# Scattering expert rows with addition into one DRAM row per token

## The chip, the cores and the metric

The kernel runs on 1 core of one Trainium2 chip. The metric is the device time of one execution in microseconds (us); lower is better. A run of the kernel before takes 539.44 us (median of 3 runs, 538.76 to 542.75).

## The reference

The input x is 8 sequences of 512 tokens with 256 numbers each, 4096 tokens in all. After a layer norm, two branches run on the same normed rows `xn`: a gated linear recurrence with its projections, whose result is `s`, and a mixture of 8 experts, of which each token uses two.

```python
logits = xn @ router_weight.T
top_vals, top_idx = jax.lax.top_k(logits, 2)
top_gates = softmax(top_vals, axis=1)
# for each expert e, with g_e the token's gate for it (0 if not chosen):
h = xn @ w_in[e].T;  a, b = split(h, 2)
acc = acc + g_e * ((silu(a) * b) @ w_out[e].T)
moe = acc + bias
out = x + s * silu(moe)
```

What matters here: each token's row of `moe` is the sum of two gated expert rows and the bias row.

## The kernel before

Engines: PE is the matrix engine, DVE the vector engine, ACT the scalar engine, POOL the general engine that issues indirect DMAs, SP the engine that only issues DMAs and waits.

**First part (0 to about 160 us).** x is loaded, normed and transposed, the tokens are routed, and the recurrence branch runs chunk by chunk (8 chunks of 512 tokens). Meanwhile SP brings in the expert weights in 24 pieces of 512 KB (`load_w`, L298 to L305, L314), POOL scatters every token's normed row twice into a DRAM table sorted by expert, `slots_dram` (64 indirect DMAs of 128 rows, L424). A row there is 256 numbers and 4 of metadata: expert, two parts of the gate, and the token's number in a form that gives the destination row (`tok_row`). Slots without a token are filled with a row whose destination is out of bounds (`NO_ROW`, L370), so that its result is written nowhere.

**Expert part (about 160 to 500 us).** 39 blocks: 32 of 256 slots ("pair blocks", `units(b)` is 2) and 7 of 128 slots ("single blocks"). `b` is the block and `i = b % 2` the half of each double buffer. For a block:
- SP, `load_slots` (L321): waits until `meta` of block b-2 is done (`meta_ready >= b-1`, L324), then loads the block's slots (L326).
- PE, `one_block(b)` (L1143): `hidden` half 0 of block b (into bankA), the transposes of block b+1's slots (L1112, need its load), `hidden` half 1 (bankB), then `outputs` of block b-1 (bankC).
- ACT and DVE apply silu, the product and the split into high and low halves between them.
- DVE, `gate_y(b)` (L917): `ys = outputs * gate + half_bias`, one instruction for each 128 rows (L924), and signals `y_sb`.
- POOL, in program order `meta(b)`, `scatter_y(b-1)`, `meta(b+1)`, `scatter_y(b)`, and so on. `meta(b)` (L442 to L462) waits for `y_scattered[i]`, that is until the scatter of block b-2 has landed (L447), and works out gate and destination of each slot in seven small instructions. `scatter_y(b)` (L464 to L473) waits for `y_sb` and issues one indirect DMA (L470) for each 128 rows into `y_dram`.

`y_dram` has two rows per token, 8192 in all. A token's first choice goes to its even row and its second choice to its odd row. Each of them holds half the bias, so that their sum holds it whole. The half bias is made by a small load and one ACT instruction (L625, L631, L632).

**Tail (about 500 us to the end).** When the last scatters have landed (L349), SP loads `y_dram` in 8 chunks of 1 MB, both rows of each token (L352). For each chunk: DVE adds the two rows (`sum_y`, L957), ACT takes silu (L646), DVE multiplies by `s` (`finish`, L963) and adds x (`add_x`, L970), SP stores 512 KB (L355). DVE's order is sum 0, sum 1, finish 0, sum 2, finish 1, add 0, and so on.

Of the kernel before, what the change touches and what calls it, by code (L numbers as in the profile page):

```python
# [43 lines left out]
BLOCK = 256  # L44
SB = BLOCK // P
# [8 lines left out]
META = 4  # L54
# [13 lines left out]
MASKED = -3.0e38  # L68
ROWS_OUT = TOPK * T
NO_ROW = float(ROWS_OUT + 1)  # L70
N_SCATTERS = TOPK * NT
# [12 lines left out]
def units(b):  # L84

    return SB if not isinstance(b, int) or b < PAIRS else 1


def scatters_before(b, i):

    if not isinstance(b, int):
        return b if i == 0 else b - 1
    return sum(units(a) for a in range(i, b, 2))


def build(nc, x, wq, wv, wg, wo, beta, ln_g, ln_b, router, w_exp, bias, out):
    ctx = ExitStack()
    with ctx:
# [3 lines left out]
        def sem(name):  # L102
            return ctx.enter_context(nc.semaphore(name))
# [3 lines left out]
        y_dram = nc.dram_tensor("y_dram", (ROWS_OUT, D), F32).ap()  # L107
# [4 lines left out]
        w_raw = sb("w_raw", [P, E * EW])  # L112
# [4 lines left out]
        rows_raw = sb("rows_raw", [P, NT * ROW])  # L117
# [11 lines left out]
        def part(raw, words):  # L129
            at[0] += words  # L130
            return raw[:, at[0] - words:at[0]]

        def recurrence_buffers(raw):
# [19 lines left out]
              for _ in range(2)]  # L153
# [6 lines left out]
        ys = [part(rows_raw, SB * D).rearrange("p (s d) -> p s d", d=D) for _ in range(2)]  # L160
        half_bias = part(rows_raw, D)
        is_first, gate_c, dest_f = [[part(rows_raw, SB) for _ in range(2)] for _ in range(3)]
        dest = [part(rows_raw, SB).bitcast(I32) for _ in range(2)]
# [3 lines left out]
        at[0] = 0  # L167
        y_in = [part(w_raw, TPC * TOPK * D).rearrange("p (t c d) -> p t c d", t=TPC, c=TOPK)
                for _ in range(CH)]
        x_late = part(w_raw, (CH - X_EARLY) * TPC * D).rearrange("p (t d) -> p t d", d=D)  # L170
        assert at[0] <= E * EW
        res = [a[:, :, 0, :] for a in y_in]

# [22 lines left out]
        tok_row = routing((NT,), "t")  # L196
# [17 lines left out]
        fill32 = sb("fill32", [P, ROW])  # L214
# [23 lines left out]
        def slots_ps_of(b, i):  # L238
# [3 lines left out]
        x_loaded = [sem(f"x_loaded{i}") for i in range(2)]  # L242
        rt_loaded, wat_loaded, cols_loaded, bias_loaded = map(
            sem, ("rt_loaded", "wat_loaded", "cols_loaded", "bias_loaded"))
# [3 lines left out]
        lam_th, lam_ready, bias_halved = sem("lam_th"), sem("lam_ready"), sem("bias_halved")  # L248
        wat_hi_ready, wat_lo_ready = sem("wat_hi_ready"), sem("wat_lo_ready")
# [22 lines left out]
        y_loaded = [sem(f"y_loaded{c}") for c in range(CH)]  # L272
        moe_sum, moe_silu, gated, dve_added = map(
            sem, ("moe_sum", "moe_silu", "gated", "dve_added"))
# [4 lines left out]
        y_v = y_dram.rearrange("(t p c) d -> p t c d", p=P, c=TOPK)  # L279
        slots_v = slots_dram.rearrange("(n p) r -> p n r", p=P)  # L280
# [6 lines left out]
        def _(sp):  # L287
# [16 lines left out]
            for c in range(3):  # L304
                load_w(c)  # L305
# [54 lines left out]
        def _(pool):  # L360
            n = [0]

            def step(ins):

                n[0] += 1
                ins.then_inc(pool_step, 1)
                pool.wait_ge(pool_step, n[0])

            step(pool.memset(fill32[:, :], 0.0))
            step(pool.memset(fill32[:, D + META - 1:D + META], NO_ROW))  # L370
            pool.nop().then_inc(consts, 1)
# [20 lines left out]
            for g in range(AHEAD - 1):  # L392
# [3 lines left out]
                      allow_small_or_imprecise_dtypes=True)  # L396
            pool.iota(tok_row[:, :], [[2 * P, NT]], base=1, channel_multiplier=2,
                      allow_small_or_imprecise_dtypes=True)
# [43 lines left out]
            def meta(b, i, first):  # L442

                pool.wait_ge(slot_loaded[i], b * 8 + 16 if i == 0 else b * 8 + 8)
                if not first:
                    pool.wait_ge(y_sb, b - 1)
                    pool.wait_ge(y_scattered[i], 16 * scatters_before(b, i))  # L447
                e_b = blk_e[:, bass.ds(b, 1)].to_broadcast([P, SB])
                pool.tensor_tensor(is_first[i][:, :], slot_in[i][:, :, D], e_b, ALU.subtract)\  # L449
                    .then_inc(pool_step, 1)  # L450
                pool.wait_ge(pool_step, b * 3 + n_meta + 1)

                pool.tensor_tensor(spare[:, i:i + 1], spare[:, 6:7], spare[:, 6:7], ALU.add)  # L453
# [3 lines left out]
                pool.tensor_tensor(gate_c[i][:, :], slot_in[i][:, :, D + 1], is_first[i][:, :], ALU.mult)  # L457
# [6 lines left out]
            def scatter_y(b, i):  # L464
# [12 lines left out]
            meta(1, 1, True)  # L477
            scatter_y(0, 0)
            with pool.Fori(2, PAIRS - 1, 2) as b:
# [11 lines left out]
        def _(act):  # L491
# [132 lines left out]
            recur(CH - 1, convert=False, last=True)  # L624
            act.dma_start(half_bias, bias).then_inc(bias_loaded, 16)  # L625
            half(0, 0, 0, 0)
# [3 lines left out]
            high_slots(1, 1, True)  # L630
            act.wait_ge(bias_loaded, 16)  # L631
            act.activation(half_bias, half_bias, ACT.Copy, scale=0.5).then_inc(bias_halved, 1)  # L632
            half(1, 1, 0, 1)
# [16 lines left out]
        def _(dve):  # L650
            n = [0]

            def step(ins):

                n[0] += 1
                ins.then_inc(route_step, 1)
                dve.wait_ge(route_step, n[0])
# [283 lines left out]
            halves(1, 1)  # L941
            dve.wait_ge(bias_halved, 1)
            gate_y(0, 0, True)
# [27 lines left out]

            sum_y(0)
            for c in range(CH):
                if c + 1 < CH:
                    sum_y(c + 1)
                finish(c)
                if c >= 1:
                    add_x(c - 1)
# [236 lines left out]
```

## Time and profile before

| what | us |
|---|---|
| time, median of 3 runs | 539.44 |
| time of the profiled execution | 541.56 |
| its span, first to last instruction | 539.7 |
| PE busy | 440.1 |
| DVE busy | 317.6 |
| POOL busy | 235.9 |
| ACT busy | 218.2 |
| last scatter issued | 497.95 |
| first load of `y_dram` issued | 500.50 |
| first instruction of the tail on DVE | 505.93 |
| last instruction of DVE | 534.69 |

The granted clock of TensorE was 0.924 of full speed on average, and full from 200 to 490 us. Times of the rows are counted from the span's start. Busy time is counted per engine, and engines overlap. What sets the time is the chain of work that ended last, in which each piece waited for the one before it.

### The profile page before, as it was taken

Reading aid. Unit: us, or ns where it says so; the run is one execution under the profiler, and the core shown is the slowest. Engines: PE = TensorE matmul, PEld = TensorE weight load, DVE = VectorE, ACT = ScalarE, POOL = GpSimd, SP = SyncE. Lnnn points to the kernel's source line nnn. Section 1 sums busy time; section 2 is a strip of 40 time slices with the busy share of each in tenths; the row PEclk is TensorE's granted clock in tenths of the full one; section 3 lists DMA queues with packets and bytes.
Section 4 is the critical chain, followed back from the end, with each engine's and each line's share of the span. In section 5 each row is a group of like instructions: output and inputs, shape, how many; then the busy total and the mean of one; then the engine's idle time right before and its main releaser. Section 6 shows DMA issues by size and latency. Waiting matters only on the chain.

```text
span 539.7 us, 12930 instructions
## 1 busy us (share of the span) xinstructions
PE 440.1 (82%) x3798; PEld 352.1 (65%) x3799; DVE 317.6 (59%) x609; ACT 218.2 (40%) x355; POOL 235.9 (44%) x536
## 2 busy tenths in 40 slices
PE   1766796979985999999999999999999997886000
PEld 1643454636544888888888888888888886664000
DVE  4898999969944245454454544545445444332397
ACT  4863366577546233333242332423323332221131
POOL 4717876877832043434444344443444344434000
PEclk9659898989989799999999999999999999999555
DMA  8802539966121214422212122121221211101897
GB/s 263 279 7 100 174 130 304 313 235 227 69 79 49 79 51 127 149 63 95 59 59 68 49 78 59 59 67 49 77 58 60 63 47 56 36 22 27 300 386 259
DMA packets 40824, 63.83 MB, mean 118 GB/s; under 512 B 4701, under 2 KB 29536, under 8 KB 40800
## 3 DMA queue, kind: packets, MB, share of 16 engines
q1 hardware_dynamic: 32512, 45.41, 27.0%
q0 software_dynamic: 6480, 16.92, 8.8%
q10 hardware_dynamic: 1808, 1.19, 0.7%
q8 instruction: 14, 0.23, 0.2%
q14 instruction: 10, 0.08, 0.0%
HBM read 40.00 MB, written 24.42 MB: 119 GB/s over the span
## 4 chain that ended last, share of the span: by engine, by line
issue 38%; DMA 23%; POOL 17%; DVE 11%; ACT 4%; PE 3%; POOLq 2%; DVEq 0%; SPq 0%; ACTq 0%
DMA y_dram<-rows_raw 17%; POOL slots_dram L424 3%; POOL y_dram L470 2%; DVE w_raw L848 2%; PE bankC L988 2%; DMA w_raw<-y_dram 2%; DMA work<-w_exp_in 2%; DMA w_raw<-x_in 2%; ACT w_raw L561 2%; POOL rows_raw L461 1%; POOL spare L453 1%; POOL rows_raw L449 1%; POOL spare L468 1%; POOL rows_raw L457 1%; POOL rows_raw L454 1%
## 5 line engine op out<-in xcount | busy, mean ns | idle before, releaser
L988 PE MATMUL bankA<-rows_raw,w_raw 128*128 128x256 f16 (+1 forms) x936 | 105.6, 268 | 7.2 <-DVE rows_raw L904 5.7
L988 PE MATMUL bankC<-w_raw,rows_raw 128*128 x852 | 100.1, 273 | 5.0 <-issue 5.0
L988 PE MATMUL bankB<-rows_raw,w_raw 128*128 128x256 f16 (+1 forms) x936 | 103.7, 264 | 0.1
L988 PEld LDWEIGHTS bankA<-rows_raw,w_raw 128*128 x936 | 87.3, 99 | 21.0 <-issue 9.2
L988 PEld LDWEIGHTS bankB<-rows_raw,w_raw 128*128 x936 | 86.8, 97 | 11.0 <-issue 0.2
L988 PEld LDWEIGHTS bankC<-w_raw,rows_raw 128*128 128x128 f16 x852 | 81.3, 98 | 18.1 <-issue 7.3
L424 POOL DMA_INDIRECT slots_dram<-rows_raw,pos_i x64 | 74.6, 1166 | 29.9 <-issue 18.5
L470 POOL DMA_INDIRECT y_dram<-rows_raw x71 | 72.5, 1021 | 30.7 <-issue 30.7
L914 DVE TENSOR_TENSOR rows_raw<-rows_raw 128x512 f16<-128x512 f32 (+1 forms) x78 | 50.3, 645 | 52.4 <-ACT rows_raw L613 52.4
L910 DVE SCALAR_TENSOR_TENSOR rows_raw<-rows_raw,bankA 128x512 f32<-128x512 f32 (+1 forms) x39 | 25.0, 640 | 93.9 <-ACT rows_raw L608 93.9
L608 ACT ACTIVATE rows_raw<-bankA 128x512 f32<-128x512 f32 (+1 forms) x39 | 21.8, 559 | 130.4 <-PE bankA L988 130.4
L613 ACT ACTIVATE rows_raw<-rows_raw 128x512 f16<-128x512 f32 (+1 forms) x78 | 46.1, 591 | 56.2 <-DVE rows_raw L910 56.2
L468 POOL TENSOR_TENSOR spare<-spare 128x1 f32<-128x1 f32 x39 | 7.5, 193 | 105.4 <-DVE rows_raw L924 105.3
L910 DVE SCALAR_TENSOR_TENSOR rows_raw<-rows_raw,bankB 128x512 f32<-128x512 f32 (+1 forms) x39 | 25.0, 640 | 21.6 <-ACT rows_raw L608 21.5
L924 DVE SCALAR_TENSOR_TENSOR rows_raw<-bankC,rows_raw 128x256 f32<-128x256 f32 x71 | 31.4, 480 | 7.0 <-PE bankC L988 4.1
L449 POOL TENSOR_TENSOR rows_raw<-rows_raw,blk_e 128x2 f32<-128x2 f32 x39 | 7.7, 197 | 61.0 <-DMA y_dram<-rows_raw 61.0
L608 ACT ACTIVATE rows_raw<-bankB 128x512 f32<-128x512 f32 (+1 forms) x39 | 21.8, 559 | 28.7 <-PE bankB L988 28.7
L848 DVE SCALAR_TENSOR_TENSOR w_raw<-work,w_raw 128x1024 f32 (+1 forms) x24 | 27.8, 1215 | 1.1 <-ACT w_raw L561 0.9
L1112 PE MATMUL bankD<-ident,rows_raw 128*128 128x128 f32 x138 | 22.4, 281 | 5.4 <-DMA rows_raw<-slots_dram 5.1
L904 DVE TENSOR_TENSOR rows_raw<-bankD,rows_raw 128x512 f16<-128x512 f32 (+1 forms) x38 | 24.1, 635 | 2.6 <-ACT rows_raw L600 2.6
L561 ACT ACTIVATE w_raw<-work 128x1024 f32 (+1 forms) x24 | 23.8, 1048 | 4.3 <-DMA work<-w_exp_in 4.3
L588 ACT ACTIVATE work<-bankD,stat 128x256 f32<-128x256 f32 x32 | 15.4, 563 | 19.3 <-POOL stat L389 19.3
(160 smaller groups left out, 604.7 us busy)
## 6 DMA issues: line engine op xcount, KB each, us to landing
work<-w_exp_in SPq DMA_DIRECT2D x24, 512.0 KB, 5.4
rows_raw<-slots_dram SPq DMA_DIRECT2D x32, 260.0 KB, 2.7
w_raw<-y_dram SPq DMA_DIRECT2D x8, 1024.0 KB, 13.5
w_raw<-x_in SPq DMA_DIRECT2D x9, 512.0 KB, 4.5
out<-w_raw SPq DMA_DIRECT2D x8, 512.0 KB, 4.2
work<-x_in SPq DMA_DIRECT2D x7, 512.0 KB, 4.4
slots_dram<-fill SPq DMA_DIRECT2D x9, 260.0 KB, 5.9
y_dram<-rows_raw POOLq DMA_INDIRECT x71, 2.5
```

The source lines that it names most:

```text
L424: pool.indirect_dma_start(out=slots_dram, out_offset=bass.IndirectOffsetOnAxis(slot, 0), in_=row, in_offset=None, bounds_check=SLOTS - 1, ...
L470: pool.indirect_dma_start(out=y_dram, out_offset=bass.IndirectOffsetOnAxis(dest[i][:, s:s + 1], 0), in_=ys[i][:, s, :], in_offset=None, bo ...
L561: act.activation(w_hi[:, bass.ds((c * PIECES + i) * PIECE, PIECE)], wst[:, i % STAGES, :], ACT.Copy, scale=WSCALE).then_inc(w_hi_ready, 1)
L608: act.activation(sil[j][:, :, 0:n], AB[j][:, :, 0:n], ACT.Silu, scale=1.0 / WSCALE).then_inc(sil_ready, 1)
L613: act.activation(g_hi[i][:, 2 * j:2 * j + 2, 0:n], g32[j][:, :, 0:n], ACT.Copy)\
L848: dve.scalar_tensor_tensor(w_lo[:, piece], wst[:, i % STAGES, :], WSCALE, w_hi[:, piece], ALU.mult, ALU.subtract).then_inc(w_lo_ready, 1)
L904: dve.tensor_tensor(xT[i][:, KD:2 * KD, 0:n], slots_ps_of(b, i)[:, :, 0:n], xT[i][:, 0:KD, 0:n], ALU.subtract).then_inc(slot_lo_ready, 1)
L910: dve.scalar_tensor_tensor(g32[j][:, :, 0:n], sil[j][:, :, 0:n], 1.0 / WSCALE, AB[j][:, :, BLOCK:BLOCK + n], ALU.mult, ALU.mult).then_inc( ...
L914: dve.tensor_tensor(g_lo[i][:, 2 * j:2 * j + 2, 0:n], g32[j][:, :, 0:n], g_hi[i][:, 2 * j:2 * j + 2, 0:n], ALU.subtract).then_inc(g_split, 1)
L924: last = dve.scalar_tensor_tensor(ys[i][:, s, :], bankC[:, i, s * D:s * D + D], gate_c[i][:, s:s + 1], half_bias, ALU.mult, ALU.add)
L988: last = pe.matmul(out_ap, lhsT, rhs, start=(n == 0), stop=(n == len(todo) - 1))
L1112: last = pe.transpose(slots_ps_of(b, i)[:, k, s * P:s * P + P], slot_in[i][:, s, k * P:k * P + P], ident32[:, :])
```

## The change

- `y_dram` gets one row per token (4096) and 128 more rows at the end for slots without a token: 4224 rows. `tok_row` is the token's number, and the filler row's destination is 4096 plus its partition, made by an iota in place of a memset.
- After the first 4 pieces of weights, SP sets all of `y_dram` to the bias with 5 DMAs from DRAM to DRAM.
- `gate_y` leaves the bias out: it becomes a product with a per-row scalar. The load and the scaling of `half_bias` go.
- `meta` loses the instruction that subtracts `is_first` from the destination (L458), since both choices go to the same row.
- `scatter_y` adds into DRAM (`compute_op=ALU.add`), with `oob_is_err=True`. A scatter now waits until the scatter of the block before it has landed as well (`y_scattered[1 - i]`), and the first one until the bias is in place. Two additions into one row must not overlap.
- In the tail a chunk of `y_dram` is 512 KB. `sum_y` is gone, and ACT waits for the load itself.

```diff
+            load_w(0)
+            for t in range(0, NT, 2 * TPC):
+                sp.dma_start(y_v[:, t:t + 2 * TPC, :], bias.unsqueeze(1).to_broadcast([P, 2 * TPC, D]))\
+                  .then_inc(y_started, 16)
+            sp.dma_start(y_v[:, NT, :], bias).then_inc(y_started, 16)
+            for c in range(1, 3):
                 load_w(c)
...
             for c in range(CH):
-                sp.dma_start(y_in[c], y_v[:, c * TPC:(c + 1) * TPC, :, :]).then_inc(y_loaded[c], 16)
+                sp.dma_start(res[c], y_v[:, c * TPC:(c + 1) * TPC, :]).then_inc(y_loaded[c], 16)
...
-                pool.tensor_tensor(dest_f[i][:, :], slot_in[i][:, :, D + 3], is_first[i][:, :], ALU.subtract)\
...
-                pool.tensor_copy(dest[i][:, :], dest_f[i][:, :]).then_inc(meta_ready, 1)
+                pool.tensor_copy(dest[i][:, :], slot_in[i][:, :, D + 3]).then_inc(meta_ready, 1)
...
+            def scatter_y(b, i, first=False):
                 pool.wait_ge(y_sb, b + 1)
                 pool.wait_ge(meta_ready, b + 1)
+                if first:
+                    pool.wait_ge(y_started, 16 * (NT // (2 * TPC) + 1))
+                else:
+                    pool.wait_ge(y_scattered[1 - i], 16 * scatters_other(b, i))
...
                     pool.indirect_dma_start(
                         out=y_dram, out_offset=bass.IndirectOffsetOnAxis(dest[i][:, s:s + 1], 0),
-                        in_=ys[i][:, s, :], in_offset=None,
-                        bounds_check=ROWS_OUT - 1, oob_is_err=False).then_inc(y_scattered[i], 16)
+                        in_=ys[i][:, s, :], in_offset=None, bounds_check=ROWS_OUT - 1,
+                        oob_is_err=True, compute_op=ALU.add).then_inc(y_scattered[i], 16)
...
-                act.wait_ge(moe_sum, c + 1)
+                act.wait_ge(y_loaded[c], 16)
...
-                    last = dve.scalar_tensor_tensor(ys[i][:, s, :], bankC[:, i, s * D:s * D + D],
-                                                    gate_c[i][:, s:s + 1], half_bias,
-                                                    ALU.mult, ALU.add)
+                    last = dve.tensor_scalar(ys[i][:, s, :], bankC[:, i, s * D:s * D + D],
+                                             gate_c[i][:, s:s + 1], None, ALU.mult)
...
-            def sum_y(c):
-                dve.wait_ge(y_loaded[c], 16)
-                dve.tensor_tensor(res[c], y_in[c][:, :, 0, :], y_in[c][:, :, 1, :], ALU.add)\
-                   .then_inc(moe_sum, 1)
```

## Rows read from the trace of the kernel before

**Rows 1.** Page, busy time of each engine: us, share of span, instructions.
```profile
PE 440.1 (82%) x3798; PEld 352.1 (65%) x3799; DVE 317.6 (59%) x609; ACT 218.2 (40%) x355; POOL 235.9 (44%) x536
```

**Rows 2.** Page, the chain that ended last: shares of the span.
```profile
issue 38%; DMA 23%; POOL 17%; DVE 11%; ACT 4%; PE 3%; POOLq 2%; DVEq 0%; SPq 0%; ACTq 0%
```

**Rows 3.** Chain in order of time, 337 to 366 us: start, length, what.
```profile
346.30 2.42 DMA y_dram<-rows_raw
...
349.80 0.15 POOL rows_raw L458
...
350.34 2.42 issue
```

**Rows 4.** Timeline, 340 to 366 us and SP from 347: start, length, instruction, [idle before].
```profile
343.26 0.88 DVE L924 SCALAR_TENSOR_TENSOR rows_raw<-bankC,rows_raw 128x256 f32<-128x256 f32 x2
345.70 0.42 PEld L1112 LDWEIGHTS bankD<-ident,rows_raw 128*128 128x128 f32 x4 [0.24 <-DMA rows_raw<-slots_dram]
354.04 0.47 PEld L1112 LDWEIGHTS bankD<-ident,rows_raw 128*128 128x128 f32 x4
360.13 0.88 DVE L924 SCALAR_TENSOR_TENSOR rows_raw<-bankC,rows_raw 128x256 f32<-128x256 f32 x2
...
351.21 0.38 SPq L326 DMA_DIRECT2D rows_raw<-slots_dram  x1
```

**Rows 5.** DMA issues by line: KB each, median us to landing; queue q0's total.
```profile
q0 software_dynamic: 6480, 16.92, 8.8%
...
rows_raw<-slots_dram SPq DMA_DIRECT2D x32, 260.0 KB, 2.7
out<-w_raw SPq DMA_DIRECT2D x8, 512.0 KB, 4.2
work<-x_in SPq DMA_DIRECT2D x7, 512.0 KB, 4.4
rows_raw<-slots_dram SPq DMA_DIRECT2D x7, 130.0 KB, 2.1
```

**Rows 6.** Page, groups of instructions: count, busy us, mean ns, idle before.
```profile
L424 POOL DMA_INDIRECT slots_dram<-rows_raw,pos_i x64 | 74.6, 1166 | 29.9 <-issue 18.5
L470 POOL DMA_INDIRECT y_dram<-rows_raw x71 | 72.5, 1021 | 30.7 <-issue 30.7
```

**Rows 7.** Timeline from 470 us: single blocks, the last scatters, the tail.
```profile
470.19 0.42 DVE L910 SCALAR_TENSOR_TENSOR rows_raw<-rows_raw,bankA 128x256 f32<-128x256 f32 x1 [2.46 <-ACT rows_raw L608]
...
496.10 1.04 POOL L470 DMA_INDIRECT y_dram<-rows_raw  x1 [0.52 <-issue]
...
497.25 0.18 POOL L468 TENSOR_TENSOR spare<-spare 128x1 f32<-128x1 f32 x1
497.95 0.99 POOL L470 DMA_INDIRECT y_dram<-rows_raw  x1 [0.51 <-issue]
500.50 13.07 SPq L352 DMA_DIRECT2D w_raw<-y_dram  x8
505.93 1.23 DVE L957 TENSOR_TENSOR w_raw<-w_raw 128x1024 f32<-128x1024 f32 x1 [8.77 <-DMA w_raw<-y_dram]
507.19 1.06 ACT L646 ACTIVATE w_raw<-w_raw 128x1024 f32<-128x1024 f32 x1 [13.22 <-DVE w_raw L957]
...
522.21 1.22 DVE L957 TENSOR_TENSOR w_raw<-w_raw 128x1024 f32<-128x1024 f32 x1
...
525.61 1.22 DVE L957 TENSOR_TENSOR w_raw<-w_raw 128x1024 f32<-128x1024 f32 x1
...
534.69 1.23 DVE L970 TENSOR_TENSOR w_raw<-w_raw 128x1024 f32<-128x1024 f32 x1
```

**Rows 8.** Stretches: length, busy of each engine, PEclk, DMA share, GB/s.
```profile
30.00:45.00 15.00, 12.21 (x170) 8.64 (x170) 12.99 (x34) 6.21 (x11) 4.09 (x4) 0.74 0.08 28
510.00:520.00 10.00, 0.00 (x0) 0.00 (x0) 9.63 (x10) 3.17 (x3) 0.00 (x0) 0.50 1.05 388
```

**Rows 9.** Waits of SP's own queue: us in total, times, longest.
```profile
SPq L302 <- DVE w_raw L848: 86.3, 16, 40.5
```

More of the change, by code:

```diff
@@ L68 @@
 MASKED = -3.0e38
-ROWS_OUT = TOPK * T
-NO_ROW = float(ROWS_OUT + 1)
+ROWS_OUT = T + P
 N_SCATTERS = TOPK * NT
@@ L93, in scatters_before, with scatters_other @@
     return sum(units(a) for a in range(i, b, 2))
+def scatters_other(b, i):
+    if not isinstance(b, int):
+        return b if i == 0 else b + 1
+    return sum(units(a) for a in range(1 - i, b, 2))
 def build(nc, x, wq, wv, wg, wo, beta, ln_g, ln_b, router, w_exp, bias, out):
@@ L160, in build @@
         ys = [part(rows_raw, SB * D).rearrange("p (s d) -> p s d", d=D) for _ in range(2)]
-        half_bias = part(rows_raw, D)
-        is_first, gate_c, dest_f = [[part(rows_raw, SB) for _ in range(2)] for _ in range(3)]
+        is_first, gate_c = [[part(rows_raw, SB) for _ in range(2)] for _ in range(2)]
         dest = [part(rows_raw, SB).bitcast(I32) for _ in range(2)]
@@ L167, in build @@
         at[0] = 0
-        y_in = [part(w_raw, TPC * TOPK * D).rearrange("p (t c d) -> p t c d", t=TPC, c=TOPK)
-                for _ in range(CH)]
+        res = [part(w_raw, TPC * D).rearrange("p (t d) -> p t d", t=TPC) for _ in range(CH)]
         x_late = part(w_raw, (CH - X_EARLY) * TPC * D).rearrange("p (t d) -> p t d", d=D)
         assert at[0] <= E * EW
-        res = [a[:, :, 0, :] for a in y_in]
         def x_of(c):
@@ L242, in build @@
         x_loaded = [sem(f"x_loaded{i}") for i in range(2)]
-        rt_loaded, wat_loaded, cols_loaded, bias_loaded = map(
-            sem, ("rt_loaded", "wat_loaded", "cols_loaded", "bias_loaded"))
+        rt_loaded, wat_loaded, cols_loaded, y_started = map(
+            sem, ("rt_loaded", "wat_loaded", "cols_loaded", "y_started"))
         wst_loaded = [sem(f"wst_loaded{i}") for i in range(STAGES)]
@@ L247, in build @@
         rt_hi, rt_split = sem("rt_hi"), sem("rt_split")
-        lam_th, lam_ready, bias_halved = sem("lam_th"), sem("lam_ready"), sem("bias_halved")
+        lam_th, lam_ready = sem("lam_th"), sem("lam_ready")
         wat_hi_ready, wat_lo_ready = sem("wat_hi_ready"), sem("wat_lo_ready")
@@ L272, in build @@
         y_loaded = [sem(f"y_loaded{c}") for c in range(CH)]
-        moe_sum, moe_silu, gated, dve_added = map(
-            sem, ("moe_sum", "moe_silu", "gated", "dve_added"))
+        moe_silu, gated, dve_added = map(sem, ("moe_silu", "gated", "dve_added"))
         stored = sem("stored")
@@ L278, in build @@
         out_v = out.rearrange("(t p) d -> p t d", p=P)
-        y_v = y_dram.rearrange("(t p c) d -> p t c d", p=P, c=TOPK)
+        y_v = y_dram.rearrange("(t p) d -> p t d", p=P)
         slots_v = slots_dram.rearrange("(n p) r -> p n r", p=P)
@@ L303, in load_w @@
                         "p a w -> p (a w)")).then_inc(wst_loaded[i % STAGES], 16)
-            for c in range(3):
+            load_w(0)
[4 more added lines that the diff above has]
+            for c in range(1, 3):
                 load_w(c)
@@ L369, in _ @@
             step(pool.memset(fill32[:, :], 0.0))
-            step(pool.memset(fill32[:, D + META - 1:D + META], NO_ROW))
+            step(pool.iota(fill32[:, D + META - 1:D + META], [[1, 1]], base=T, channel_multiplier=1,
+                           allow_small_or_imprecise_dtypes=True))
             pool.nop().then_inc(consts, 1)
@@ L396, in _ @@
                       allow_small_or_imprecise_dtypes=True)
-            pool.iota(tok_row[:, :], [[2 * P, NT]], base=1, channel_multiplier=2,
+            pool.iota(tok_row[:, :], [[P, NT]], base=0, channel_multiplier=1,
                       allow_small_or_imprecise_dtypes=True)
@@ L456, in meta @@
                 pool.wait_ge(pool_step, b * 3 + n_meta + 2)
-                pool.tensor_tensor(gate_c[i][:, :], slot_in[i][:, :, D + 1], is_first[i][:, :], ALU.mult)
-                pool.tensor_tensor(dest_f[i][:, :], slot_in[i][:, :, D + 3], is_first[i][:, :], ALU.subtract)\
+                pool.tensor_tensor(gate_c[i][:, :], slot_in[i][:, :, D + 1], is_first[i][:, :], ALU.mult)\
                     .then_inc(pool_step, 1)
@@ L461, in meta @@
                 pool.tensor_tensor(gate_c[i][:, :], gate_c[i][:, :], slot_in[i][:, :, D + 2], ALU.add)
-                pool.tensor_copy(dest[i][:, :], dest_f[i][:, :]).then_inc(meta_ready, 1)
-            def scatter_y(b, i):
+                pool.tensor_copy(dest[i][:, :], slot_in[i][:, :, D + 3]).then_inc(meta_ready, 1)
+            def scatter_y(b, i, first=False):
                 pool.wait_ge(y_sb, b + 1)
                 pool.wait_ge(meta_ready, b + 1)
+                if first:
+                    pool.wait_ge(y_started, 16 * (NT // (2 * TPC) + 1))
+                else:
+                    pool.wait_ge(y_scattered[1 - i], 16 * scatters_other(b, i))
                 pool.tensor_tensor(spare[:, 2 + i:3 + i], spare[:, 6:7], spare[:, 6:7], ALU.add)
@@ L477, in _ @@
             meta(1, 1, True)
-            scatter_y(0, 0)
+            scatter_y(0, 0, True)
             with pool.Fori(2, PAIRS - 1, 2) as b:
@@ L624, in _ @@
             recur(CH - 1, convert=False, last=True)
-            act.dma_start(half_bias, bias).then_inc(bias_loaded, 16)
             half(0, 0, 0, 0)
@@ L630, in _ @@
             high_slots(1, 1, True)
-            act.wait_ge(bias_loaded, 16)
-            act.activation(half_bias, half_bias, ACT.Copy, scale=0.5).then_inc(bias_halved, 1)
             half(1, 1, 0, 1)
@@ L941, in _ @@
             halves(1, 1)
-            dve.wait_ge(bias_halved, 1)
             gate_y(0, 0, True)
@@ L970, in add_x @@
                 dve.tensor_tensor(res[c], res[c], x_of(c), ALU.add).then_inc(dve_added, 1)
-            sum_y(0)
             for c in range(CH):
-                if c + 1 < CH:
-                    sum_y(c + 1)
                 finish(c)
```

## Prediction

> **What bounds the kernel now.** I read the page's busy times first [rows 1]. PE is busy 82% of the span, and one expects the matrix engine to be the bound. The chain that ended last says otherwise [rows 2]: PE holds 3% of it, POOL 17%, DMA 23%, and "issue" (nobody in the view to wait for) 38%. So I laid out one round of the expert part from the chain in order of time [rows 3] and the timeline [rows 4]. The reader is to follow one loop:
>
> - `gate_y` of a block starts at 343.26 and takes 0.88 for its two instructions.
> - POOL issues the second of its two scatters at 346.30. It lands 2.42 later, at 348.7.
> - `meta` of the block two further on waits for that landing and ends at 350.34.
> - SP waits for that `meta`, and issues the slot load at 351.21, 0.87 later (its wait, and reading the row number).
> - PE starts the transposes that need this load at 354.04, 2.83 after the issue, where a load of this size takes 2.7 to land [rows 5]. That leaves about 0.1. In the other parity PE stands idle for the load: 0.24 before the transposes at 345.70.
> - After the transposes come `hidden` half 1 and `outputs`, and the `gate_y` two blocks after the first starts at 360.13.
>
> The loop is 360.13 - 343.26 = 16.87 us for two blocks, and nothing in it is spare. PE alone would need only some 0.24 less per two blocks. So PE and the round trip through POOL, the scatter's landing, `meta` and SP bind at once. Any time added between `gate_y` and the slot load makes two blocks longer by that time; any time taken out gives at most 0.24. POOL itself is not full: it idles 2.42 after `meta` [rows 3].
>
> How many rounds: block b+4's load hangs on block b's scatter. It holds from about block 2's scatter to block 33's gate, 31 blocks or 15.5 rounds; I count 15, since one parity starts with a few tenths in hand. The single blocks at the end have one scatter each and some 1 us in hand.
>
> The tail is bound elsewhere. 24 DVE instructions of 128x1024 run from 505.93 to 535.92 [rows 7]. In mid tail the sums start at 522.21 and 525.61, so three instructions take 3.40, 1.13 each. DMA is full at the same time, 388 GB/s [rows 8]: after the change one of the two could turn out to be the limit.
>
> **The change part by part.** The durations are of the profiled execution (541.56, span 539.7), 2.1 above the median of 539.44; I put the difference on the median.
>
> *Tail.* Before: first load issued at 500.50, first DVE instruction 5.43 later. After: a chunk is 512 KB instead of 1 MB. Half of it less at 388 GB/s is 1.35, so the first one lands about 4.1 after the first issue, silu takes 1.06, and DVE starts at 5.3. Its 16 instructions take 16 x 1.13 = 18.1, and some 0.3 is lost while the second chunk is awaited. DVE ends at 23.7; before it was 35.4. That is 11.7 less; I take 11.5. DMA does not take over: 8.4 MB in place of 12.6 MB at 388 GB/s is 21.6, plus the first landing less than the 27.3 that the tail then lasts. Loads with rows of 1 KB could run slower than these of 2 KB; x comes in with 1 KB rows, and its 512 KB take 4.4 like the 4.2 of the stores [rows 5].
>
> *New wait at the end.* In the loop the wait for the other half's scatter costs nothing: POOL's program has `meta(b+1)` between `scatter_y(b-1)` and `scatter_y(b)`, and it waits for that very landing already. Only the last scatter has no `meta` before it. Before, it went out at 497.95, while the one before was still under way (issued 496.10). After, it waits until 496.10 + 2.55 = 498.65 and then takes the 0.70 from the small addition at 497.25 to the scatter [rows 7]: 499.35. That is +1.4, and behind it are queued the loads of all the tail. It also shows two landings bare, so an addition's extra landing time counts there twice.
>
> *Addition instead of writing.* No row shows it. Two unknowns: e, the longer issue on POOL, and d, the later landing. Per round of a pair block e counts twice and d once.
> - Lowest: both zero. The bytes that POOL handles are the same.
> - e highest: the issue takes twice as long, +1.0 on 1.02 [rows 6]. Nearest row: the same instruction with other rows and more going on around it, L424, takes 1.17, +0.15. I take 0.15.
> - d highest: the old rows are first read, then added and written. A read of 130 KB takes 2.1 from issue to landing [rows 5]. If the read runs beside the source's, 130 KB more cost what 260 KB cost over 130 KB in the same load, 2.7 - 2.1 = 0.6. Reading DRAM instead of writing it makes 4.4 from 4.2, +0.2. I take 0.8.
> - So 2 x 0.15 + 0.8 = 1.1 per round, and 0.95 for a single scatter.
>
> A third way to d: by queue q0's total [rows 5], 131 KB took 8.8% x 539.7 x 131 / 16920 = 0.37 us of all engines. If an addition only moves the read bytes twice, the landing comes 0.37 later and the round grows by 2 x 0.15 + 0.37 = 0.67, 0.52 for a single scatter; the sum is then 15 x 0.42 - 11.5 + 1.4 + 1.04 = -2.8. I take 0.8 since a load's landing grew by more than its bytes.
>
> The Trainium skill ("Collectives: The Full Stack", section "The bandwidth ceiling: the fold count and why AG ≠ RS ≠ AR") says that a reducing DMA is slower because it reads two sources, not because of the adding. By that it would be 536.6 in place of 544.0. No row of the kernel before shows an adding DMA.
>
> *Taken out of the round.* L458 is 0.15 on POOL [rows 3]. `gate_y` reads one operand less: 0.88 for two, while a DVE instruction with 256 numbers takes 0.42 at the least in the rows [rows 7], so 0.05, up to 0.1. Together 0.25 at best, which I take.
>
> *Hidden.* SP's five bias DMAs write 4.3 MB. They stand ahead of the second group of weights, which is held up to 40.5 us by DVE anyway [rows 9], and DMA is at 0.08 of its capacity from 30 to 45 us [rows 8]; 4.3 MB read and written are at most 22 us at 388 GB/s. Without that cover it would be these 22 us. The first expert scatter, which waits for them, comes over 100 us later. `half_bias` on ACT, iota for memset, 896 filler rows more written: nothing, they lie beside a busy PE or a scatter that is issued anyway.
>
> **The sum.** Per round 1.1 - 0.25 = +0.85, times 15 = +12.8. Tail -11.5, new wait +1.4, twice 0.95 = +1.9. In all +4.6: 539.4 + 4.6 = 544.0. The gain in the tail is paid back in the loop. It turns at a round extra of about 0.8, below which the kernel is faster.
>
> **Rivals.**
> 1. *Adding is nearly free* (extra below 0.7 per round). For it: the small share of DMA in the loop, the same number of indices. With zero: the round can shrink by only 0.24, -3.6; -11.5 + 1.4 - 3.6 = -13.7, 525.7. With the bytes read twice and no more, 0.67: -2.8, 536.6; 0.10 of this rival's chance. At 0.7 (single 0.6): 6.75 - 10.1 + 1.2 = -2.2, 537.2. This ends on the other side and decides from 0.8 down.
> 2. *Adding is dear* (above 1.5): each row is read, added and written in its own turn, or POOL prepares half as many entries again. At 1.5 (single 1.25): 18.75 - 10.1 + 2.5 = +11.2, 550.6. At read-then-write, 2.1 + 0.3 = 2.4: 32.3 - 10.1 + 4.5 = +26.7, 566. Against it: POOL's 2.42 idle says that even then no second loop closes.
> 3. *The loop does not bind* because SP's load could be late by more than I read: PE's 0.24 idle would come from something else. Then only the tail counts: -11.5 + 1.4 + 1.9 = -8.2, 531.2. Against it: the transposes follow the load by 2.7 to 2.8 in both parities, the time of its landing.
>
> **From chances to numbers.** Forecast (extra 0.7 to 1.5: 537.2 to 550.6) 0.45; rival 1 0.27; rival 2 0.20; rival 3 0.08. A change under 1% (5.4 us) is not told from none in this kernel. Faster than 534.0 needs an extra below 0.47: two thirds of rival 1 and all of rival 3, with some rounding 0.27. Slower than 544.8 begins at 1.16: rival 2 and nearly half of the forecast, 0.40. Within: 0.33. The range for 8 in 10 goes from 529 (an extra of 0.2) to 559 (an extra of 2.0). For the forecast alone it is 537 to 551.
>
> **What the new profile would show.** Two `gate_y` of one parity 17.7 apart instead of 16.87; the scatter's landing at about 3.3 to 3.4 after its issue instead of 2.42; the DMA_INDIRECT at 1.15 to 1.2; PE idle before the transposes, over 0.5 per block. In the tail no DVE sum, 16 instructions, and 27 to 28 from the first load's issue to the end. The last scatter goes out only after the one before has landed. I am wrong if the landing stays near 2.4 (rival 1), if it is past 4 (rival 2), if the landing is late and the period is not (rival 3), or if the tail's DMA keeps DVE waiting.

## The result and the profile after

| | before | after |
|---|---|---|
| time, median (range) | 540.14 (538.76 to 542.75) | 583.12 (576.84 to 589.49) |
| time of the profiled execution, its span | 541.56, 539.7 | 581.51, 579.7 |
| ratio to before, with its interval | | 1.0749 [1.0672, 1.0827] |

The run of 589.49, over 1.5% above the fastest of its kernel, is left out of the ratio and of the comparisons below; the other three have a median of 581.51. The change makes the kernel 7.5% slower, about 41 us. The forecast was slower by 4.6 us, with a range up to 559, so the sign is right and the size is far off.

The page of the changed kernel, busy times first, then the slices, the costliest groups, and the DMA issues (us to landing last):

```profile
PE 458.6 (79%) x3798; PEld 364.3 (63%) x3799; DVE 309.5 (53%) x601; ACT 219.4 (38%) x354; POOL 274.7 (47%) x497
...
PEclk9998897998898999998899889889999999898855
...
L482 POOL DMA_INDIRECT y_dram<-rows_raw x71 | 113.0, 1592 | 30.7 <-issue 30.7
...
L1111 PE MATMUL bankD<-ident,rows_raw 128*128 128x128 f32 x138 | 23.5, 291 | 36.8 <-DMA rows_raw<-slots_dram 36.0
...
w_raw<-y_dram SPq DMA_DIRECT2D x8, 512.0 KB, 7.5
```

POOL's indirect DMA takes 1.59 us instead of 1.02 [rows 6]. PE, which hardly ever waited for a slot load before, now waits 36.0 us for them. Its busy time has grown by 18.5 us with the same number of matmuls, and PEclk shows an 8 again and again through the loop where it was 9: it computes more slowly as well as later.

One round of the loop [rows 3, 4] in the changed kernel. First the chain in order of time:

```profile
333.08 3.69 DMA y_dram<-rows_raw
...
341.40 3.65 DMA y_dram<-rows_raw
```

The landing comes 3.65 to 3.69 after the second scatter's issue, against 2.42. Over all 71 scatters, the least, the median and the most from issue to landing, before and then after:

```profile
DMA to landing us min/median/max: 2.2/2.5/3.7
...
DMA to landing us min/median/max: 3.6/3.8/5.1
```

Then the timeline of the same stretch:

```profile
329.53 0.88 DVE L933 TENSOR_SCALAR rows_raw<-bankC,rows_raw 128x256 f32<-128x256 f32 x2
...
331.18 1.59 POOL L482 DMA_INDIRECT y_dram<-rows_raw  x1 [0.51 <-issue]
...
332.28 2.78 PE L987 MATMUL bankB<-rows_raw,w_raw 128*128 128x256 f16 x24
...
333.08 1.58 POOL L482 DMA_INDIRECT y_dram<-rows_raw  x1 [0.31 <-issue]
...
336.95 0.18 POOL L457 TENSOR_TENSOR rows_raw<-rows_raw,blk_e 128x2 f32<-128x2 f32 x1 [2.28 <-DMA y_dram<-rows_raw]
337.21 0.65 POOL L461 TENSOR_TENSOR spare<-spare 128x1 f32<-128x1 f32 x1
...
342.43 0.45 PEld L1111 LDWEIGHTS bankD<-ident,rows_raw 128*128 128x128 f32 x4 [2.40 <-DMA rows_raw<-slots_dram]
...
343.06 4.31 PE L987 MATMUL bankB<-rows_raw,w_raw 128*128 128x256 f16 x24
```

The second scatter goes out 1.90 after the first (1.37 before, up to the issue at 346.30 in [rows 3]), PE waits 2.40 for the slot load, and then 24 matmuls into bankB take 4.31, where the same 24 took 2.78 one block earlier. The small addition at L461, a part of `meta`, takes 0.65 here in an even block and 0.20 in the odd block after it. The stretches of the same time, with the granted clock as the third number from the right, before DMA's share and GB/s:

```profile
332.00:335.00 3.00, 3.00 (x30) 2.72 (x28) 1.47 (x3) 1.71 (x3) 2.36 (x2) 1.00 0.37 44
343.00:346.00 3.00, 3.00 (x16) 2.11 (x15) 0.82 (x2) 0.60 (x1) 0.56 (x3) 0.50 0.40 49
347.00:350.00 3.00, 3.00 (x30) 2.70 (x28) 1.26 (x2) 1.23 (x2) 0.00 (x0) 1.00 0.33 89
```

After the idle stretch the granted clock is 0.50, 1.2 GHz, and then it is full again, 2.4 GHz. This one costs 4.31 - 2.78 = 1.53 us, on top of the wait.

The tail, from the timeline:

```profile
542.35 1.62 POOL L482 DMA_INDIRECT y_dram<-rows_raw  x1 [0.51 <-issue]
542.98 0.41 SPq L354 DMA_DIRECT2D w_raw<-x_in  x1
542.98 0.48 DVE L933 TENSOR_SCALAR rows_raw<-bankC,rows_raw 128x256 f32<-128x256 f32 x1 [1.41 <-PE bankC L987]
547.60 0.18 POOL L480 TENSOR_TENSOR spare<-spare 128x1 f32<-128x1 f32 x1 [3.63 <-DMA y_dram<-rows_raw]
548.30 1.56 POOL L482 DMA_INDIRECT y_dram<-rows_raw  x1 [0.52 <-issue]
552.10 7.26 SPq L359 DMA_DIRECT2D w_raw<-y_dram  x8
...
557.31 1.23 DVE L965 TENSOR_TENSOR w_raw<-w_raw,xs_raw 128x1024 f32<-128x1024 f32 x1 [13.84 <-ACT w_raw L655]
...
574.72 1.22 DVE L972 TENSOR_TENSOR w_raw<-w_raw 128x1024 f32<-128x1024 f32 x1
```

Where the 39.95 us between the two profiled executions are, by points of the timelines:

| part | before | after | difference |
|---|---|---|---|
| start to the gate of block 2 | 207.48 | 210.15 | +2.7 |
| gate of block 2 to gate of block 33 | 259.77 | 301.80 | +42.0 |
| gate of block 33 to that of block 38 | 29.43 | 31.03 | +1.6 |
| last gate to the first load of the tail | 3.82 | 9.12 | +5.3 |
| first load of the tail to the end | 39.2 | 27.6 | -11.6 |

### The profile page after: what moved, and what is told of

Same layout as the page of the kernel before. It is cut to its first block, busy times and chain, and to the rows that moved or that the text cites. A ratio compares the mean times of both kernels' runs of the same rounds, so it can differ in the third digit from the quotient of the medians.

```text
span 579.7 us, 12886 instructions
## 1 busy us (share of the span) xinstructions
PE 458.6 (79%) x3798; PEld 364.3 (63%) x3799; DVE 309.5 (53%) x601; ACT 219.4 (38%) x354; POOL 274.7 (47%) x497
## 3 DMA queue, kind: packets, MB, share of 16 engines
q0 software_dynamic: 13296, 17.83, 18.1%
## 4 chain that ended last, share of the span: by engine, by line
issue 33%; DMA 28%; POOL 17%; DVE 10%; PE 7%; POOLq 2%; ACT 1%; DVEq 0%; SPq 0%; ACTq 0%
DMA y_dram<-rows_raw 26%; PE bankC L987 2%; POOL y_dram L482 2%; POOL spare L461 2%; POOL slots_dram L432 2%; PE bankA L987 2%; DVE w_raw L857 2%; DMA w_raw<-x_in 2%; POOL rows_raw L457 1%; POOL stat L396 1%; POOL rows_raw L465 1%; POOL rows_raw L462 1%; POOL spare L480 1%; DVE work L848 1%; DVE w_raw L965 1%
## 5 line engine op out<-in xcount | busy, mean ns | idle before, releaser
L482 POOL DMA_INDIRECT y_dram<-rows_raw x71 | 113.0, 1592 | 30.7 <-issue 30.7
L987 PE MATMUL bankB<-rows_raw,w_raw 128*128 128x256 f16 (+1 forms) x936 | 117.3, 287 | 0.1
L987 PEld LDWEIGHTS bankB<-rows_raw,w_raw 128*128 x936 | 95.0, 107 | 16.5 <-issue 0.3
L987 PEld LDWEIGHTS bankC<-w_raw,rows_raw 128*128 128x128 f16 x852 | 82.7, 98 | 15.8 <-issue 5.4
L432 POOL DMA_INDIRECT slots_dram<-rows_raw,pos_i x64 | 71.7, 1120 | 30.8 <-issue 20.7
L1111 PEld LDWEIGHTS bankD<-ident,rows_raw 128*128 128x128 f32 x138 | 15.5, 143 | 42.3 <-DMA rows_raw<-slots_dram 41.8
L933 DVE TENSOR_SCALAR rows_raw<-bankC,rows_raw 128x256 f32<-128x256 f32 x71 | 31.4, 479 | 5.8 <-PE bankC L987 5.4
L857 DVE SCALAR_TENSOR_TENSOR w_raw<-work,w_raw 128x1024 f32 (+1 forms) x24 | 27.6, 1213 | 0.0
L612 ACT ACTIVATE rows_raw<-bankD 128x512 f16<-128x512 f32 (+1 forms) x38 | 20.8, 548 | 14.8 <-PE bankD L1111 14.6
```

The lines of the kernel that those rows point to most:

```text
L432: pool.indirect_dma_start(out=slots_dram, out_offset=bass.IndirectOffsetOnAxis(slot, 0), in_=row, in_offset=None, bounds_check=SLOTS - 1, ...
L482: pool.indirect_dma_start(out=y_dram, out_offset=bass.IndirectOffsetOnAxis(dest[i][:, s:s + 1], 0), in_=ys[i][:, s, :], in_offset=None, bo ...
L612: act.activation(xT[i][:, 0:KD, 0:n], slots_ps_of(b, i)[:, :, 0:n], ACT.Copy)\
L857: dve.scalar_tensor_tensor(w_lo[:, piece], wst[:, i % STAGES, :], WSCALE, w_hi[:, piece], ALU.mult, ALU.subtract).then_inc(w_lo_ready, 1)
L933: last = dve.tensor_scalar(ys[i][:, s, :], bankC[:, i, s * D:s * D + D], gate_c[i][:, s:s + 1], None, ALU.mult)
L987: last = pe.matmul(out_ap, lhsT, rhs, start=(n == 0), stop=(n == len(todo) - 1))
```

## The experiments

In the table "loop" is the time from the gate of block 2 to that of block 33 (259.8 before, 301.8 after), a round is two blocks, and a slow round is one of 19.8 us or more, of the 13 between the gates of blocks 4 and 30; the usual round is the median of the others. Loops and rounds are of one profiled execution each. The kernel before took 539.8 to 540.6 beside them.

| kernel | time | ratio to before | usual round | slow rounds | loop |
|---|---|---|---|---|---|
| before | 540.1 | | 16.9 | 0 | 259.8 |
| after | 581.5 | 1.075 | 18.8 | 8 | 301.8 |
| write instead of add | 531.1 | 0.983 [0.979, 0.987] | 16.9 | 0 | 260.5 |
| short filler | 547.7 | 1.014 [1.011, 1.018] | 17.2 | 0 | 265.3 |
| long filler | 560.2 | 1.035 [1.032, 1.039] | 18.1 | 1 | 278.6 |
| double filler | 570.8 | 1.057 [1.050, 1.063] | 18.3 | 1 | 287.4 |
| filler in even blocks | 590.0 | 1.091 [1.085, 1.096] | 18.8 | 9 | 304.3 |
| no wait in the loop | 582.8 | 1.082 [1.075, 1.090] | 18.9 | 7 | 302.0 |
| flag off (one run) | 570.4 | | 18.8 | 4 | 294.7 |
| split loads, added | 525.2 | 0.972 [0.968, 0.976] | 16.6 | 0 | 251.5 |
| split loads, old scatter | 531.1 | 0.984 [0.979, 0.989] | 16.6 | 0 | 251.4 |
| split loads, write instead of add | 521.9 | 0.967 [0.962, 0.972] | 16.6 | 0 | 251.5 |
| split loads, x load last | 524.0 | 0.969 [0.966, 0.972] | 16.6 | 0 | 252.3 |

**1. The addition taken out.**

```diff
-                        oob_is_err=True, compute_op=ALU.add).then_inc(y_scattered[i], 16)
+                        oob_is_err=True).then_inc(y_scattered[i], 16)
```

> This kernel is the changed one with the addition taken out of the scatter: it writes its rows (the output lacks one of each token's two expert rows and the bias). All waits, the bias DMAs, the short tail and the bounds flag stay. Theory A (the addition itself is the cost: 0.57 us longer on POOL per indirect DMA, and a later landing): the issue falls back from 1.59 to about 1.0, the landing from 3.7 to 2.4, a round of two blocks from 18.6 to 20.5 back to 16.7 to 16.9, no half clock between 200 and 490 us, and the time is 540.1 - 11.6 + 1.4 + up to 1.7 for a later start = about 531. Rival B (the bounds flag or the 128 more rows make the issue long): issue still 1.5 to 1.6, time 560 to 583. Rival C (the new waits or the bias DMAs cost): issue short, but time above 540.

The lines of its page:

```profile
PEclk9659898999899899999999999999999999999855
...
L482 POOL DMA_INDIRECT y_dram<-rows_raw x71 | 73.2, 1031 | 30.9 <-issue 30.9
```

and the summary of its scatters, from issue to landing:

```profile
DMA to landing us min/median/max: 2.4/2.5/4.6
```

531.1, as theory A gave. All 50 us between this kernel and the changed one come from adding in place of writing; the waits, the bias DMAs, the flag and the 128 more rows are in both. The short tail then brings what it promised.

**2. The same delay without any addition.** In `meta`, behind the small addition at L453, a filler that nobody reads:

```diff
+                pool.iota(delay, [[1, 860]], base=0, channel_multiplier=0,
+                          allow_small_or_imprecise_dtypes=True)
```

> This kernel is the one before with a filler instruction on POOL in each block's meta, about 1.75 us long (an iota over 860 numbers that nobody reads). Nothing is added in DRAM, the tail is the old one. It puts the same delay into the round trip as the addition does (1.8 us per two blocks). Theory A (the loop binds, and the idle PE then loses its clock): the round grows from 16.87 to at least 18.5, the granted clock falls to half for some 3.4 us in many rounds as in the changed kernel, and the time is 540.1 + 15.5 x 1.75 = 567 without the clock, 575 to 585 with it. Rival B (the delay alone explains everything and the clock belongs to something else): 567 with full clock. Rival C (the loop has slack): under 545.

> As the long delay, but the filler is about 0.7 us long (340 numbers). Theory A (linear in the delay, and the clock falls only from some idle time on): round 17.5, time 540.1 + 15.5 x 0.7 = 551, clock full from 200 to 490 us. Rival B (any added idle makes the clock fall): 555 to 565 with half clock in many rounds. Rival C (slack in the loop): under 543.

The filler was shorter than I had reckoned, 0.85 us and, with 340 numbers, 0.42. So the long one doesn't match the addition's delay, and neither kernel gave its forecast time. What they do show is the slope. With the short one `meta` took 0.4 longer, a round grew by about 0.33 and the loop by 5.6. With the long one `meta` of an even block took 2.8 instead of 1.45 (the filler, and a slower instruction behind it), a round grew by 1.2 and the loop by 18.8, that is 15.5 x 1.2 = 18.6. So the loop has only some 0.1 us of slack per round, and what goes beyond it counts in full. Between the gates of blocks 4 and 30 the clock stayed full but for one round.

**3. The double filler.** The same filler twice in each `meta`.

> This kernel is the one before with two fillers on POOL in each block's meta, each the 860-number iota that took 0.85 us in the long delay and made a round 1.2 us longer (16.87 to 18.1). Nothing is added in DRAM. Theory A (an idle of 2 us of PE before the transposes, whoever causes it, lets its clock fall, as in the changed kernel): the round grows to about 19 and PE idles 2 us or more once a round; then the clock is at half for 3.4 us in most rounds, and a round is over 20.5; time 575 to 595. Rival B (the half clock of the changed kernel comes from the additions' DMA work or from chance): rounds of 19 with full clock, 540.2 + 15.5 x 2.1 = 573 or less.

570.8. The time is rival B's, but the condition that was to be tested did not come about: the usual round was 18.3, and PE's wait fell on both blocks of a round.

```profile
332.63 0.42 PEld L1117 LDWEIGHTS bankD<-ident,rows_raw 128*128 128x128 f32 x4 [1.32 <-DMA rows_raw<-slots_dram]
341.41 0.42 PEld L1117 LDWEIGHTS bankD<-ident,rows_raw 128*128 128x128 f32 x4 [0.55 <-DMA rows_raw<-slots_dram]
```

Only one of the 13 rounds was slow. A round that is 1.5 us longer doesn't by itself bring the clock down.

**4. The filler in even blocks alone.** A power of 8 numbers, 1.67 us:

```diff
+                if i == 0:
+                    pool.tensor_tensor(delay, fill32[:, 0:8], fill32[:, 0:8], ALU.pow)
```

> This kernel is the one before with one filler on POOL (a power of 8 numbers, reckoned at 1.9 us from the 1.04 us that 4 take) in the meta of even blocks alone. Nothing is added in DRAM. The double delay spread PE's idle time over both blocks of a round (1.3 and 0.3 us); here it should stand in one stretch of about 2 us before the transposes, as in the changed kernel. Theory A (the long single idle stretch makes the clock fall, once a round): half clock in at least 6 rounds between 200 and 480 us, 576 to 590 us. Rival B (it needs the additions): full clock nearly throughout, round 18.6 to 18.9, 566 to 572 us.

590.0: theory A, without one addition in DRAM. Its page and its timeline:

```profile
PEclk9998898998998998999889989988998899899655
...
L473 POOL DMA_INDIRECT y_dram<-rows_raw x71 | 73.1, 1030 | 30.4 <-issue 30.4
```

```profile
343.43 0.71 PEld L1115 LDWEIGHTS bankD<-ident,rows_raw 128*128 128x128 f32 x4 [2.60 <-DMA rows_raw<-slots_dram]
...
344.34 3.86 PE L991 MATMUL bankB<-rows_raw,w_raw 128*128 128x256 f16 x24
...
353.71 2.78 PE L991 MATMUL bankB<-rows_raw,w_raw 128*128 128x256 f16 x24
```

The scatters are the old ones (1.03 us). PE idles 2.60 in one stretch, and the 24 matmuls after it take 3.86 instead of 2.78. Nine of 13 rounds are slow. So the half clock needs no addition in DRAM; it comes with one long idle stretch of PE in each round. It isn't certain to follow. In the changed kernel the weight loads wait 2.2 to 2.7 in the eight slow rounds and 2.0 to 2.6 in those at full clock, of which this is one, with its stretch:

```profile
404.37 0.42 PEld L1111 LDWEIGHTS bankD<-ident,rows_raw 128*128 128x128 f32 x4 [2.44 <-DMA rows_raw<-slots_dram]
...
404.00:408.00 4.00, 3.63 (x33) 3.30 (x34) 1.38 (x2) 1.22 (x3) 1.45 (x4) 1.00 0.53 61
```

The Trainium skill ("TensorE: Matmul & The Clock Gate", section "HAM oscillation — how this bites in real kernels") describes a matmul kernel whose clock falls again and again because a wait for DMA is repeated in each tile. The changed kernel's trace agrees in its eight slow rounds, with 0.50 granted after the wait of 2.40, and not in the others, with 1.00 granted after the wait of 2.44.

**5. Two parts of the change that could have been the cause.** The wait on the other half's scatter left out, except at the last block:

```diff
-                else:
+                elif isinstance(b, int) and b == BLOCKS - 1:
                     pool.wait_ge(y_scattered[1 - i], 16 * scatters_other(b, i))
```

> This kernel is the changed one without the new wait on the other half's scatter, except at the last block, where it stays. Meta of the next block already waits for that landing, so the order of the additions is the same. Theory A (the new wait costs nothing in the loop): the time of the changed kernel, 583 +- 6. Rival B (the wait costs in every block): faster by more than 10 us.

582.8 against 581.5, and the loop 302.0 against 301.8: the wait costs nothing in the loop, since `meta` of the next block has waited for that landing.

And the flag back to `oob_is_err=False`, with the addition:

> This kernel is the changed one with the bounds flag as before (an index out of bounds would be skipped). Theory A (the addition makes POOL's instruction long): 1.59 us per indirect DMA, time 583 +- 7. Rival B (the flag does): 1.0 to 1.2 us, and a time about 15 x 1 us lower.

```profile
L482 POOL DMA_INDIRECT y_dram<-rows_raw x71 | 113.0, 1592 | 30.8 <-issue 30.8
```

The instruction stays at 1.59: the flag isn't it. The time, 570.4, is a single one, below the 583 +- 7 expected and below the range of the changed kernel. Its usual round is 18.8, as there, but only 4 of the 13 are slow instead of 8. The four missing are worth 4 x 1.7 = 6.8 of the 11 us, and block 2's gate came 3.2 earlier (206.9 against 210.15). Whether the flag plays a part in that, one run can't say.

**6. The loop cut open.** The slot load becomes two. The 256 numbers that PE transposes wait for the buffer alone; the 4 numbers of metadata go to a small tile `slot_m`, with a semaphore of their own, and wait for `meta`:

```diff
                     sp.wait_ge(slot_t_ps, b - 1)
-                    sp.wait_ge(meta_ready, b - 1)
...
-                sp.dma_start(slot_in[i][:, 0:units(b), :], slots_v[:, bass.ds(row, units(b)), :])\
+                sp.dma_start(slot_in[i][:, 0:units(b), :], slots_v[:, bass.ds(row, units(b)), 0:D])\
                   .then_inc(slot_loaded[i], 16)
+                if not isinstance(b, int) or b >= 2:
+                    sp.wait_ge(meta_ready, b - 1)
+                sp.dma_start(slot_m[i][:, 0:units(b), :], slots_v[:, bass.ds(row, units(b)), D:ROW])\
+                  .then_inc(meta_loaded[i], 16)
```

> This kernel is the changed one with the slot load in two: the 256 numbers of each slot are loaded as soon as PE has transposed the buffer's last content, and only the 4 numbers of metadata, in tiles and with a semaphore of their own, wait for meta of block b-2. The scatter's landing and meta are then no longer ahead of PE's transposes. Theory A (the whole loss is the loop through the slot load): POOL's own round of 7.8 us fits below PE's 8.3, blocks go back to 8.3, PE's clock is full from 200 to 490 us, and the time is about 530 (540.1 - 11.6 tail + 5.3 around the last scatters - 0.15 x 31 = 4.5 less in the loop, +1.7 start = 531). Rival B (adding DMAs slow other traffic or POOL becomes the bound): 545 to 575.

> This kernel is the one before with the slot load in two, the metadata apart, as in the split version of the changed kernel; scatter, bias and tail are the old ones. Theory A (the loop through the slot load binds the kernel before as well, by the 0.24 to 0.29 us that PE idles per two blocks, and more around the single blocks): blocks at 8.30, time 540.2 - 4.5 - 1 = about 535. It then also says what the change brings in the tail alone: the split changed kernel took 525.2. Rival C (PE alone bound the kernel before): 540 +- 1. Rival D (the extra small DMAs cost on SP): above 541.

> This kernel is the split version of the changed one with writes in place of additions (its output lacks one expert row of each token and the bias). It prices the additions where the loop no longer carries them. Theory A (only the two bare landings after the last gate still pay): 525.2 - 2 x 1.25 = 522.7. Rival B (POOL's later scatters and the additions' DMA work still cost in the loop): below 520.

With the additions: 525.2, faster than both kernels of the case. Its page and timeline:

```profile
PEclk9659898989989799999999999999999999999755
...
L487 POOL DMA_INDIRECT y_dram<-rows_raw x71 | 113.3, 1596 | 26.0 <-issue 26.0
```

```profile
341.70 0.60 PE L1116 MATMUL bankD<-ident,rows_raw 128*128 128x128 f32 x4
342.13 2.78 PE L992 MATMUL bankB<-rows_raw,w_raw 128*128 128x256 f16 x24
342.93 1.58 POOL L487 DMA_INDIRECT y_dram<-rows_raw  x1 [0.30 <-issue]
344.75 2.78 PE L992 MATMUL bankC<-w_raw,rows_raw 128*128 x24
...
347.14 0.56 POOL L462 TENSOR_TENSOR rows_raw<-rows_raw,blk_e 128x2 f32<-128x2 f32 x1 [2.63 <-DMA y_dram<-rows_raw]
347.37 2.78 PE L992 MATMUL bankA<-rows_raw,w_raw 128*128 128x256 f16 x24
```

The additions are as long as ever, 1.60, and `meta` still waits 2.63 for their landing. But PE goes from one group of 24 matmuls to the next without a gap, at full clock, 8.3 per block. The loop falls from 301.8 to 251.5. I had expected 531: the loop is 3.8 shorter than reckoned, and the start, for which I had added 1.7, is not later than before (block 2's gate at 206.6, 207.5 before).

The kernel before with the same split takes 531.1, 9.5 less than without (I expected 5). The loop is 8.3 shorter: 3.1 from eleven ordinary rounds with 0.28 each, 1.3 from the block before gate 6, beside which x is loaded (9.6, now 8.29), 0.7 from the one before gate 26, and 3.3 from the last blocks of the loop (gates 29 to 32), where the single blocks begin. So the loop bound the kernel before as well. And on top of a kernel in which it doesn't bind, the change brings 531.1 - 525.2 = 5.9 us.

With writes in place of the additions the split kernel takes 521.9 (expected 522.7): the additions still cost 3.3. From the last gate to the first load of the tail it is 9.1 with additions and 6.5 with writes, 2.6 of the 3.3.

**7. The landing before last.**

```diff
             sp.wait_ge(y_ps, BLOCKS)
-            sp.dma_start(x_late, x_v[:, X_EARLY * TPC:, :]).then_inc(x_late_loaded, 16)
...
             for c in range(CH):
                 sp.dma_start(res[c], y_v[:, c * TPC:(c + 1) * TPC, :]).then_inc(y_loaded[c], 16)
+            sp.dma_start(x_late, x_v[:, X_EARLY * TPC:, :]).then_inc(x_late_loaded, 16)
...
+                if c >= X_EARLY:
+                    dve.wait_ge(x_late_loaded, 16)
```

> This kernel is the split version of the changed one with the 512 KB load of the last chunk of x issued after the loads of the tail, and only the last chunk's addition waits for it. In the changed kernel that load is issued at 542.98, 0.6 us after the last scatter but one (542.35), which lands 5.2 us after its issue where the others take 3.6 to 3.8. Theory A (the load delays that landing): it falls to 3.8, 525.2 - 1.3 = 523.9. Rival B (the landing is long for another reason, or the load costs as much at its new place): 525 +- 0.5.

```profile
487.90 1.62 POOL L487 DMA_INDIRECT y_dram<-rows_raw  x1 [0.51 <-issue]
491.96 0.18 POOL L485 TENSOR_TENSOR spare<-spare 128x1 f32<-128x1 f32 x1 [2.44 <-DMA y_dram<-rows_raw]
```

The last scatter but one is now followed 4.06 later by the next instruction; with the load beside it, it was 5.11. So the load did delay the landing, by about 1 us, and from the last gate to the first load of the tail it is 8.0 instead of 9.1. The time is 524.0 (521.5 to 525.8) against 525.2 (523.6 to 527.3). The two intervals overlap, so the gain in the whole is not shown.

## Why the prediction was wrong

Two terms of the sum failed: the longer issue on POOL, e, was put at 0.15 and measured 0.57 (15 x 2 x 0.42 = 13 us), and the half clock of PE behind its repeated wait was not in the sum at all and costs about 14 us. Point by point:

- **What bounds the kernel: right.** The loop through POOL, the landing, `meta` and SP had hardly any slack [rows 3, 4]. The fillers lengthen the loop of the expert part with a slope of about 15.5 per us of round, and the split removes it. Rival 3 (the loop does not bind) fell. The 0.24 that I gave as the most that could be won per round was about right for the ordinary rounds, 16.87 to 16.59, but I had missed what the loop costs in the block next to the loads of x and in its last blocks.
- **The tail: right.** 27.6 from the first load to the end, forecast 27 to 28; DMA didn't take over.
- **The landing as such: right.** I took d = 0.8. The median landing came 1.3 later after the issue (3.8 against 2.5), of which 0.57 is the longer instruction itself, so 0.7 to 0.8 is the rest.
- **The issue: wrong.** I took e = 0.15, from the spread of the same instruction between two lines [rows 6]. It is 0.57, midway between that and the bound of 1.0. The spread was no measure for another kind of work. Per round the extra is 2 x 0.57 + 0.8 = 1.9 instead of 1.1.
- **Taken out of the round: wrong.** `gate_y` takes 0.88 for two as before. Dropping an operand from this DVE instruction, which reads PSUM, saved nothing. `meta` is 0.15 shorter in odd blocks (1.30) but 0.25 longer in even blocks (1.7), since the small addition at L461 takes 0.55 there instead of 0.19; why is open. From a gate to the end of the `meta` that hangs on it, it is now 2.1 longer in even blocks and 1.75 in odd ones. The longer one, less the loop's slack, sets the round: 16.87 to 18.8, that is +1.9 where the sum had +0.85.
- **Rival 2 came, and not by its sign.** The extra of 1.9 lies in its domain, above 1.5, with a chance of 0.20. Its own prices (550.6 at 1.5, 566 at 2.4) make about 557 of 1.9. I had looked for it in a landing past 4; the landing stayed at 3.8, and 1.14 of the extra was in POOL's instructions.
- **The step that was missing: PE's clock.** Of the 42.0 us that the loop grew, 8 slow rounds with 1.7 more than the usual round each are 14, and the other 28 are the rounds at full clock (15 x 1.9). The two kernels with other numbers of slow rounds give the same 28: 34.9 - 4 x 1.7 with the flag off, 44.5 - 9 x 1.8 with the filler in even blocks. I had PE idle over 0.5 in each block; it idled 2.0 to 2.7 in every second one and not in the others. Without the clock the sum would have ended near 566, still above the range. A sum that prices a wait of PE at its length is too low once the wait is long and in one stretch. The times of the changed kernel's runs go with their mean clocks (576.84 at 0.926, 581.51 at 0.919, 584.72 at 0.908); that they differ by their number of slow rounds is not shown.
- **The last scatters: half.** I gave 3.3 for the new wait and the two bare landings; it was 5.3. The wait was mis-sized. I let the landing before last come 2.55 after its issue at 496.10, but in the trace before it took 3.6, beside the 512 KB load of x (from issue to landing):

```profile
DMA to landing us min/median/max: 3.6/3.6/3.6
```

With 3.6 the wait comes to about 2.5 instead of 1.4. The kernels with writes show it without any addition: from the last gate to the first load of the tail 7.45 against 3.8, and 6.5 against 3.9 with split loads, so 2.7 to 3.6. The additions bring 1.7 to 2.6 more, where I had 1.9. In the changed kernel that landing took 5.1, about 1 of it because of the load (experiment 7).

- **Hidden: right as to size, open in part.** Block 2's gate came 2.7 later in the changed kernel, of which the loop already had about 1. In the four other kernels with additions, which have the same bias DMAs, it came at 205.5 to 207.6, and in the kernel with writes, which has them too, at 205.1, before the 207.48 of the kernel before. The bias DMAs cost nothing that can be seen.
- **The forecast with the landing 0.37 later** (the bytes read twice and no more) was further off than mine. The landing grew by 0.7 to 0.8 beyond the issue. The rule of the Trainium skill ("Collectives: The Full Stack", section "The bandwidth ceiling: the fold count and why AG ≠ RS ≠ AR"), that a reducing DMA is slower because of its second read, does not cover the 0.57 on POOL.

With the prices of this profile the sum is 28 (rounds) + 14 (clock) + 1.6 + 2.7 + 5.3 - 11.6 = 40.0, the difference of the profiled executions. Against the forecast of +4.6 the rounds were 15 too low, the clock 14, the single blocks and last scatters together 3.6 and the start 2.7.

Not settled: why an idle stretch of 2.0 to 2.7 us brings the clock down in some rounds and not in others, and whether the flag changes how often.

## What to carry to other kernels

When the chain of waits runs through an engine that is 44% busy, and PE is 99% busy beside it (250 to 450 us), look for a loop in which both have hardly any slack. A longer step in it costs its whole length in each round, and a buffer or a split load that takes the step out of the loop can be worth more than the change that was planned: here 9.5 us against 5.9. Metadata and data that travel in one DMA tie the fast reader to the slow one. And price a wait of PE by its length and its clock: where the clock fell, an idle stretch of some 2.4 us cost about 1.5 us more in the matmuls behind it.

## What was not expected of the hardware

- An indirect DMA of 128 rows of 1 KB that adds takes 1.59 us on POOL instead of 1.02, and lands 3.8 after its issue instead of 2.5 (medians). Its length doesn't depend on the bounds flag.
- A filler on POOL (an iota over 860 numbers took 0.85 us, over 340 numbers 0.42, a power of 8 numbers 1.67) is a good probe for a loop's slack, but its length has to be read from the trace, not reckoned.
- The slow rounds are sticky. In the changed kernel seven came one after another, 20.4 to 20.9 us each, then three at 18.8 to 19.2.
